# Cross queries written in 16 transfers instead of 64, and an interleaved order of transposes in the third layer's attention

## The reference, cut to what matters

```python
# cross attention of L0, L1, L3
q = heads(xn @ q_w + q_b); k, v = split(context @ kv_w + kv_b)
x = x + attend(q, k, v) @ proj_w + proj_b
# attention of L2, with u = (norm(x) @ Wq) @ Wk.T / sqrt(128)
w = softmax(u @ context.T)          # 100 x 1444 per batch
evidence = w @ context              # 100 x 128, then @ Wv
```

## Time and profile before

| what | value |
|---|---|
| time of three runs, median | 6248.7 us (6243.02 to 6251.53) |
| the profiled execution, its own time | 6255.48 us |
| its span in the profile | 6253.2 us |
| PE busy | 5213.4 us (83%) |
| DVE, ACT, POOL busy | 3844.1 (61%), 3016.4 (48%), 1458.3 (23%) us |
| mean granted TensorE clock | 0.881 of full |

### The profile page before, as it was taken

How to read it: one execution, slowest core, us unless ns; L and a number is a source line. 1 busy time by engine, 2 the same in 40 slices (tenths; PEclk the granted TensorE clock), 3 DMA queues, 4 the chain that set the end, 5 groups by cost and what they waited for, 6 DMA issues and landing times. The chain is left out here.

```text
span 6253.2 us, 151177 instructions
## 1 busy us (share of the span) xinstructions
PE 5213.4 (83%) x64126; PEld 3352.7 (54%) x64126; DVE 3844.1 (61%) x7732; ACT 3016.4 (48%) x4479; POOL 1458.3 (23%) x758
## 2 busy tenths in 40 slices
PE   4838999999985849999999877779675799999998
PEld 3614555555653615666666545555353466666664
DVE  4537888888744527777777623334353577777773
ACT  2324666666652315666666532212322366666665
POOL 2024444444302022333222000000201223332220
PEclk7667999999996669999999977779766799999999
DMA  3325545555403345555555211110141555555540
GB/s 76 63 64 156 158 157 164 164 164 158 147 17 65 64 110 162 165 164 165 164 167 164 73 33 48 48 38 1 44 77 28 171 165 165 165 164 164 164 152 15
DMA packets 544827, 717.59 MB, mean 115 GB/s; under 512 B 183450, under 2 KB 457402, under 8 KB 531770
## 3 DMA queue, kind: packets, MB, share of 16 engines
q1 hardware_dynamic: 535322, 696.87, 38.4%
q10 hardware_dynamic: 8832, 11.07, 0.8%
HBM read 441.82 MB, written 264.09 MB: 113 GB/s over the span
## 5 line engine op out<-in xcount | busy, mean ns | idle before, releaser
L1247 DVE TENSOR_REDUCE maxima<-ps 100x1 f32<-100x482 f32 (+1 forms) x4608 | 2720.2, 650 | 896.3 <-PE ps L1092 886.6
L1202 ACT ACTIVATE probs<-ps 128x800 f32<-128x800 f32 (+1 forms) x2304 | 1800.5, 835 | 655.6 <-PE ps L1113 653.9
L1092 PE MATMUL ps<-kst,qst 48*100 48x482 bf16 (+1 forms) x4608 | 1117.7, 411 | 107.1 <-DMA qst<-cross_q_parts 51.3
L1299 POOL TENSOR_TENSOR kparts<-kf,zero 128x1444 bf16<-128x1444 f32 x192 | 498.3, 2595 | 2280.3 <-ACT kf L1174 2250.9
L1130 PE MATMUL ps<-probs,vals 128*9 128x100 f32 x36864 | 1012.4, 250 | 7.9 <-ACT probs L1202 0.8
L1113 PE MATMUL ps<-qst,kst 128*128 128x200 bf16 (+1 forms) x9216 | 999.6, 250 | 11.7 <-DMA qst<-nparts 5.5
L1113 PEld LDWEIGHTS ps<-qst,kst 128*128 128x128 bf16 (+1 forms) x9216 | 759.0, 98 | 251.2 <-issue 124.7
L1130 PEld LDWEIGHTS ps<-probs,vals 128*9 128x9 f32 x36864 | 734.3, 90 | 259.6 <-issue 219.2
L1092 PEld LDWEIGHTS ps<-kst,qst 48*100 48x100 bf16 x4608 | 341.7, 119 | 630.2 <-DVE maxima L1247 329.9
L1180 ACT ACTIVATE vals<-ps 128x512 f32<-128x512 f32 (+1 forms) x288 | 161.9, 562 | 467.1 <-PE ps L1075 467.1
L1064 PE MATMUL ps<-ident,ctok 128*128 128x128 f32 (+1 forms) x1152 | 195.6, 292 | 210.2 <-DMA ctok<-in_ctx_dram 108.7
(11 more groups left out here) (256 smaller groups left out, 4951.3 us busy)
## 6 DMA issues: line engine op xcount, KB each, us to landing
kst<-ctx_k_stack SPq DMA_DIRECT2D x96, 2888.0 KB
ctx_k_stack<-kparts SPq DMA_DIRECT2D x192, 541.5 KB
ctx_k_stack<-kparts SPq DMA_DIRECT2D x192, 361.0 KB
ctok<-in_ctx_dram SPq DMA_DIRECT2D x96, 704.0 KB
ctx_k_stack<-kparts SPq DMA_DIRECT2D x192, 180.5 KB
c<-in_ctx_dram SPq DMA_DIRECT2D x32, 704.0 KB
o_sums<-osb SPq DMA_DIRECT2D x96, 200.0 KB
qst<-cross_q_parts SPq DMA_DIRECT2D x1152, 12.5 KB
```

The lines of the kernel that those rows point to most:

```text
L1092: nc.tensor.matmul(ps[0:N, at:at + w], g.qst[s][row0:row0 + CROWS, j, N * e:N * e + N], g.kst[s][row0:row0 + CROWS, j, a:a + w], start=Tru ...
L1202: nc.scalar.activation(probs[kt % 2][hf][0:kts[kt], :].rearrange("p (k n) -> p k n", k=2), src, ACT.Exp).then_inc(exp_done, 1)
L1247: nc.vector.reduce_max(maxima[:, col:col + 1], ps[0:N, at:at + widths[c]], AX.X).then_inc(m_read, 1)
L1299: return nc.gpsimd.tensor_tensor(out, src, g.zero[0:src.shape[0], 0:1].to_broadcast(list(src.shape)), ALU.add)
```

## The change

The queries leave in one transfer for each half and chunk (64 partitions x 3 parts x 400 tokens), so 16 a layer. `g.qx` is laid out by chunk, and the 12 reads of a batch take a 100-token piece out of rows of 400. In the third layer's attention the turning of the context leaves `pe_scores` and the turning of the weights leaves `pe_evidence`; both become routines that turn one group. For each batch b TensorE's order is: weights of b groups 0 and 1, context of b+2 groups 0 and 1, weights group 2, context group 2, evidence of b, scores of b+2. The instructions, their operands and the orders on ACT, DVE, POOL and SP stay.

```diff
-    per = CH // N
     for c in range(NCH):
         sp.wait_ge(low, c + 1)
         for e in range(2):
-            for j in range(per):
-                b = c * per + j
-                sp.dma_start(g.qx[b, e].rearrange("t r n -> r t n"),
-                             parts[HALF * e:HALF * e + HALF, :, N * b:N * b + N]).then_inc(stored, 16)
-    sp.wait_ge(stored, 16 * 2 * B)
+            sp.dma_start(g.qx[c, e].rearrange("t r n -> r t n"),
+                         parts[HALF * e:HALF * e + HALF, :, CH * c:CH * c + CH]).then_inc(stored, 16)
+    sp.wait_ge(stored, 16 * 2 * NCH)
...
+                    src = g.qx[b // per, e, part].rearrange("(d j) n -> d j n", j=PAIRS)[:, :, N * (b % per):N * (b % per) + N]
                     for slot in range(first, first + copies):
                         at = QHALF * e + HD * slot
-                        sp.dma_start(g.qst[s][at:at + HD, :, N * e:N * e + N],
-                                     g.qx[bass.ds(b, 1), e, part].rearrange("a (d j) n -> (a d) j n", j=PAIRS)).then_inc(qst_loaded[s], 16)
+                        sp.dma_start(g.qst[s][at:at + HD, :, N * e:N * e + N], src).then_inc(qst_loaded[s], 16)
...
+        def pe_turn_context(pe, k, t):
+            b, s, r = k.b, k.s, k.r
+            if t == 0:
+                wait(pe, ctx_loaded[s], 32 * (r + 1))
+            wait(pe, t_read, 3 * b + max(t - 1, 0))
+            for i, kt in enumerate(range(4 * t, 4 * t + 4)):
+                o = T_BANK + BANK * (t % 2) + 128 * i
+                n = kts[kt]
+                ins = nc.tensor.transpose(ps[:, o:o + n], ctok[s][0:n, kt, :], g.ident[0:n, 0:n])
+            ins.then_inc(t_full, 1)
...
+        def pe_turn_weights(pe, k, t):
+            b, s, r = k.b, k.s, k.r
+            if t == 0:
+                wait(pe, p_norm, b + 1)
+            wait(pe, p_read, 3 * b + max(t - 1, 0))
+            for i, kt in enumerate(range(4 * t, 4 * t + 4)):
+                o = P_BANK + BANK * (t % 2) + N * i
+                n = kts[kt]
+                ins = nc.tensor.transpose(ps[0:n, o:o + N], pq[s][:, 128 * kt:128 * kt + n], g.ident[0:N, 0:N])
+            ins.then_inc(p_full, 1)
...
-                for i in range(loops):
-                    for u in range(1, LAG + 1):
-                        pe_evidence(pe, at(i, u))
-                        pe_scores(pe, at(i, u + 2))
+                for b in range(B):
+                    k, k2 = known(b), known(b + 2) if b + 2 < B else None
+                    for t in range(2):
+                        pe_turn_weights(pe, k, t)
+                    if k2 is not None:
+                        for t in range(2):
+                            pe_turn_context(pe, k2, t)
+                    pe_turn_weights(pe, k, 2)
+                    if k2 is not None:
+                        pe_turn_context(pe, k2, 2)
+                    pe_evidence(pe, k)
+                    if k2 is not None:
+                        pe_scores(pe, k2)
...
-    g.qx = nc.dram_tensor("cross_q_parts", (B, 2, PARTS, HALF, N), BF16).ap()
+    g.qx = nc.dram_tensor("cross_q_parts", (NCH, 2, PARTS, HALF, CH), BF16).ap()
```

More of the change, by code:

```diff
@@ L1352, in sp_stacks @@
             sp.dma_start(g.kst[s][:, :, :].rearrange("p j n -> p (j n)"), g.kscr[s]).then_inc(k_loaded[s], 16)
+            per = CH // N
             for e in range(2):
                 for part, (first, copies) in enumerate(Q_SLOTS):
+                    src = g.qx[b // per, e, part].rearrange("(d j) n -> d j n", j=PAIRS)[:, :, N * (b % per):N * (b % per) + N]
                     for slot in range(first, first + copies):
                         at = QHALF * e + HD * slot
-                        sp.dma_start(g.qst[s][at:at + HD, :, N * e:N * e + N],
-                                     g.qx[bass.ds(b, 1), e, part].rearrange("a (d j) n -> (a d) j n", j=PAIRS)).then_inc(qst_loaded[s], 16)
+                        sp.dma_start(g.qst[s][at:at + HD, :, N * e:N * e + N], src).then_inc(qst_loaded[s], 16)
         def sp_negmax(k):
@@ L1694, in _ @@
             def _(pe):
[L1695 to L1698, removed]
-                for i in range(loops):
-                    for u in range(1, LAG + 1):
-                        pe_evidence(pe, at(i, u))
-                        pe_scores(pe, at(i, u + 2))
[L1703 to L1706, removed]
+                for b in range(2):
+                    for t in range(3):
+                        pe_turn_context(pe, known(b), t)
+                    pe_scores(pe, known(b))
+                for b in range(B):
[11 more added lines that the diff above has]
+                        pe_scores(pe, k2)
             @block.scalar
```

## The result

The changed kernel takes 6032.7 us (median, 6030.4 to 6035.8) against 6249.8 us before: a ratio of 0.9655, 95% interval 0.9638 to 0.9672. The profiled execution took 6031.4 us.

The account below looks back on a forecast made before the run. It took the query stretch as bound by SP's issue count and the third layer's attention as nearly bound by TensorE, with waits and a varying clock. 6255.5 - 92 - 73 = 6090.5, less 6.8 for the median: 6084 us, range 6025 to 6135.

Parts of the forecast that it names:

- The queries: End of the query phase, three layers: stretch falls to 13.8 us, SP's issues setting the pace; -92 us, from -84 to -99.
- Rival 5: Query transfers gain nothing because an issue is priced by bytes, 2.6 us each; total 6176 us, chance 0.01.
- The readback at nothing: Cross attention's 12 transfers a batch keep their 200-byte pieces, only source rows lie 800 bytes apart; costed at nothing.
- Rival 4: Readback's spread-out source makes issues cost 1337 instead of 646 ns, 200 us lost; total 6284 us, chance 0.02.
- The step at full clock: Third layer's attention: a full-clock step falls from 12.11 to 10.7 us, between 10.4 and 11.1.
- rival 3: Third layer's context load becomes the bound, readable only 6.5 us after the evidence; 50 us lost, total 6134, chance 0.1.
- the clock's share: Third layer's attention: slow steps, 63% before, become fewer; mean step 13.0 us, -73 us over 30 steps.
- the prediction's own signs: Wrong if steady-step mean clock leaves 0.7 to 0.9, context wait mostly exceeds 2 us, or SP's negated-maxima wait disappears.
- Its own case: Whole kernel: queries -84 to -99 us, third-layer steps 12.4 to 13.6 us, total 6059 to 6110; chance 0.62.
- rival 2: TensorE's clock stays full in the third layer's attention, saving 142 us there; total 6015 us, chance 0.1.
- Rival 1: Third layer's clock does not profit or worsens; every step slow, mean 14.7 us, total 6135, chance 0.15.
- the rule beside it: Skill's clock-gate page: transposes do not count as TensorE activity like matmuls, so filling the wait would not keep clock up.

Follow-up runs that it names:

- q_only: The kernel before with only the change's query part (fewer, larger query transfers), old TensorE order kept: 6161.8 us, ratio 0.9848.
- four_slots: The changed kernel with a fourth buffer for the third layer's context tokens, so each load starts one evidence earlier: 6064.5 us, ratio 0.9697.
- idle_turns: The kernel before with eight extra context transposes, results thrown away, in TensorE's wait before weight group 2: 6203.7 us, ratio 0.9918.
- weights_first: The changed kernel with TensorE turning all three weight groups first, then all three context groups: 6065.8 us, ratio 0.9692.
- combined: The changed kernel with a fourth context buffer, ACT copying context groups 0 and 1 before the exponentials, and 8 query transfers a layer: 5972.2 us, ratio 0.9551.

## Why the prediction was right, and where its size was off

**The queries: right.** Forecast was a stretch of 13.8 us and 92 us in all; measured 13.5 and 93.5, and 93.2 alone in q_only. SP stayed the pace, the dearer landing cost 0.3 instead of 0.7 us. Rival 5 falls with it: an issue of four times the bytes takes 618 ns.

**The readback at nothing: right.** Its issues take a median of 647 ns against 646, and SP's queue still waits for the negated maxima (rows of the changed kernel beside the earlier trace rows):

```profile
L1356 SPq DMA_DIRECT2D qst<-cross_q_parts x1152: 632/647/1351, 437.0 to 5850.7; - x192
...
SPq L1365 <- DVE nparts L1268: 607.3, 96, 24.2
```

From the first context load of L0's cross attention to the next layer's query transfers 1798.25 us pass in both kernels; the stretches behind the queries of L1 and L3 are 0.6 and 2.5 us longer, most of the 3.6 us above. Rival 4 is out.

**The step at full clock: right in its parts, a little long.** Forecast 10.7 (10.4 to 11.1), measured 10.36. The evidence starts 4.7 us after the row maximum as said, and the context is turned 5.2 us after the evidence ended (3708.14 to 3713.36), inside the 4.3 to 5.3 forecast. The 0.3 us charged for the late load was not paid; four_slots shows that it is wholly covered by the wait for ACT, and rival 3 falls. A slow step takes 15.1 instead of 14.7 us.

**The term that was mis-sized is the clock's share.** "I take 13.0 us a step: 2.44 x 30 = -73 us". Measured: 10.94 us and -135. Of that, 1.75 x 30 = 53 us are the shorter full-clock step, and 82 us are the clock: above its full-clock step the mean step lay 15.44 - 12.11 = 3.33 us before and 10.94 - 10.36 = 0.58 after. In the forecast the same difference is 3.33 against 13.0 - 10.7 = 2.3, worth 31 us. The forecast took an old share of slow steps of 63% and lowered it to somewhat above a half. Only four of 30 steps ran below full clock, three at 15.2 to 15.5 us and one at 11.6.

Two readings behind that share were wrong. The old steps are not of two kinds: six take 12.11 us, eight 13.74 (clock 0.88) and sixteen 17.4 to 17.8, so the clock stayed up in 20% of the steps and not in 37%. And the old full-clock step leaves TensorE idle for 12.11 - 8.73 = 3.38 us, not 2.5 (the window over the step of the earlier trace rows, columns as in the earlier trace rows):

```profile
3927.30:3939.41 12.11, 8.73 (x57) 6.17 (x56) 4.73 (x9) 3.16 (x5) 0.35 (x1) 1.00 0.21 62
```

The runs show that the share was never a property of the stage but hung on small amounts of waiting: a wait shorter by 0.9 us moved the old order from 15.4 to 13.5 us a step, a maximum longer by 1.7 us moved the new one from 10.9 to 14.0.

By the prediction's own signs its account of the clock was wrong: it named a mean clock above 0.9 as such a sign, and 0.95 was measured. Its own case, 6059 to 6110, was missed too. The total lies in the range only because the range was stretched towards rival 2; for the third layer's attention, which gave 135 us where 73 were forecast, that is luck.

Rival 2, the clock staying full (6015), was given 0.1 and is nearest to what happened. Rival 1, every step slow, is refuted by the mean of 10.94 us, and the rule beside it, that transposes do not count, by idle_turns. The reason given for the forecast's direction, that the eight transposes fill the wait, is half wrong: the late load keeps a wait of the same length open. What went are the gaps behind it, and weights_first, whose first wait is not filled at all, keeps three quarters of the gain a step.

**What stays open.** weights_first and four_slots have the full-clock step of the changed kernel within 0.11 us and nearly the same sum of waits, and yet 0.84 and 0.83 of the clock instead of 0.95. One step at full clock of the changed kernel, weights_first, four_slots and idle_turns, in windows (columns as in the earlier trace rows):

```profile
3757.11:3767.47 10.36, 8.47 (x57) 6.20 (x56) 4.73 (x10) 3.05 (x5) 0.35 (x1) 1.00 0.26 76
3857.69:3868.16 10.47, 8.46 (x57) 6.19 (x56) 4.73 (x9) 3.16 (x5) 0.35 (x1) 1.00 0.26 72
3766.54:3776.90 10.36, 8.47 (x57) 6.14 (x56) 4.73 (x9) 3.05 (x5) 0.35 (x1) 1.00 0.10 29
3956.76:3968.87 12.11, 9.60 (x65) 7.00 (x64) 4.73 (x10) 3.16 (x5) 0.35 (x1) 1.00 0.22 63
```

TensorE idles for 1.89, 2.01, 1.89 and 2.51 us in them, and the mean clocks are 0.95, 0.84, 0.83 and 0.89. So neither the idle time of a step nor its share puts the kernels in order, and the longest single wait does not either (1.86 us in the changed kernel, 1.01 in four_slots). What decides is not shown. One candidate is the place and the splitting of the waits. Another is the rhythm: the steps of four_slots repeat a pattern, mostly one of 10.36 and two of 13.60 us, while those of the changed kernel vary by some tenths of a microsecond with the landing of the load. No run here separates the two.

## What to carry to other kernels

Where TensorE's granted clock switches between its two levels within a stage, cost the stage at both levels and ask how small a change of its waits would tip it; on this kernel that was worth more than the shorter chain itself (82 against 53 us). Removing a wait from a covered place can cost time, and wasted array work in an unavoidable wait can save it: try both when the clock is not full. Before a barrier with one engine issuing transfers, count issues before bytes, and read from a trace what one issue costs in its layout.

## What the runs showed of the hardware

Wasted work made a kernel faster: 256 extra transposes in waits, 49 us less (ratio 0.9918, 0.9904 to 0.9933), with the mean clock of the steady steps up from 0.73 to 0.89. A buffer more, which removed a load's wait, made it 27 us slower. And issuing a transfer of 300 KB over 128 partitions took SP 360 ns in the layout of combined, against 618 ns for 150 KB over 64 partitions and 513 ns for the 300 KB of line 191: neither the bytes nor the number of contiguous pieces alone sets the price of an issue, and which property of the addresses does was not tried.
